# The transfers of value tiles 4 to 7 moved into steps 4 to 7 of the loop, and the first two residual loads put behind step 3

## What is computed

```
xq  = (1 + scale_q) * norm(x)   + bias_q      # scale, bias = silu(cond) @ Wss_q + bss_q
xkv = (1 + scale_kv) * norm(ctx) + bias_kv
q = xq @ Wq + bq;  k, v = split(xkv @ Wkv + bkv)
attn = softmax(q k^T / sqrt(32))               # per head
out = x + (attn v) @ Wp + bp
```

## Time and profile before

| | |
|---|---|
| median of 3 runs | 1062.99 us (1062.55 to 1064.18) |
| the profiled execution's own time | 1062.06 us |
| its span in the profile | 1060.2 us |
| PE busy | 1019.4 us, 96% of the span |
| DVE busy | 989.8 us, 93% |
| POOL busy | 832.3 us, 79% |
| ACT busy | 787.5 us, 74% |
| granted TensorE clock over the span | 0.994 |

### The profile page before, as it was taken

The page is one execution under the profiler, slowest core; times in us unless marked ns, Lnnn a source line. Parts: engine busy times, 40 slices in busy tenths (PEclk is TensorE's granted clock), DMA queues, the critical chain, the costliest instruction groups (busy, mean ns, idle before and its releaser), DMA issues.

```text
span 1060.2 us, 29080 instructions
## 1 busy us (share of the span) xinstructions
PE 1019.4 (96%) x10051; PEld 576.6 (54%) x10051; DVE 989.8 (93%) x1288; ACT 787.5 (74%) x1400; POOL 832.3 (79%) x933
## 2 busy tenths in 40 slices
PE   6999899999999999999999999999999999999965
PEld 2666555555555555555555555555555555555532
DVE  5775899999999999999999999999999999999994
ACT  2564677878787887878787878878787878877552
POOL 2372587979888897979898888979797988889454
PEclk8999999999999999999999999999999999999999
DMA  9231478877777778777777777777777777776775
GB/s 346 102 100 51 99 175 190 178 191 183 182 193 175 184 172 197 184 176 188 194 174 183 189 182 189 169 194 183 177 188 185 183 191 177 184 191 142 160 159 129
DMA packets 382386, 185.19 MB, mean 175 GB/s; under 512 B 324828, under 2 KB 328952, under 8 KB 382344
## 3 DMA queue, kind: packets, MB, share of 16 engines
q1 hardware_dynamic: 382320, 184.66, 71.4%
q10 hardware_dynamic: 24, 0.01, 0.0%
HBM read 77.90 MB, written 33.55 MB: 105 GB/s over the span
## 4 chain that ended last, share of the span: by engine, by line
PE 75%; DMA 7%; SPq 7%; DVE 4%; issue 4%; POOL 2%; ACT 0%; POOLq 0%; DVEq 0%; ACTq 0%
PE ps_q L1442 26%; PE ps_o L1503 26%; PE ps_s L1465 8%; PE ps_v L1487 8%; DMA pt<-p 6%; PE ps_v L1425 4%; SPq L369 3%; SPq L358 2%; DMA cx<-in_ctx_dram 1%; PE ps_v L1296 1%; SPq L334 1%; DVE v L1023 1%; DVE p L1107 0%; DVE cx L932 0%; PE ps_s L1367 0%
## 5 line engine op out<-in xcount | busy, mean ns | idle before, releaser
L527 POOL TENSOR_TENSOR xr<-y,xr 128x512 f32<-128x512 f32 x128 | 163.0, 1273 | 57.5 <-ACT y L667 55.7
L691 ACT CAST p<-ps_t 128x1024 f16<-128x1024 f32 x128 | 129.5, 1012 | 100.0 <-DVE ps_t L1083 98.3
L534 POOL TENSOR_TENSOR half_den<-pr 128x512 f32<-128x512 f32 x128 | 163.4, 1277 | 51.1 <-ACT pr L726 49.0
L503 POOL TENSOR_TENSOR xr<-xr,bp_row 128x512 f32<-128x512 f32 x128 | 163.0, 1273 | 0.8 <-DMA xr<-in_x_dram 0.8
L1091 DVE TENSOR_REDUCE mx<-ps_s 128x16 f32<-128x1024 f32 x128 | 156.8, 1225 | 7.1 <-PE ps_s L1465 2.8
L1107 DVE TENSOR_TENSOR p<-ps_t,p 128x1024 f16<-128x1024 f32 x128 | 156.6, 1223 | 4.0 <-ACT p L691 2.7
L1083 DVE SCALAR_TENSOR_TENSOR ps_t<-pr,ps_v 128x1024 f32<-128x1024 f32 x128 | 155.8, 1217 | 0.3
L1099 DVE TENSOR_TENSOR pr<-ps_s,mx 128x1024 f32<-128x1024 f32 x128 | 155.6, 1215 | 0.1
L726 ACT ACTIVATE pr<-pr,exp_scale 128x1024 f32<-128x1024 f32 x128 | 146.3, 1143 | 10.6 <-DVE pr L1099 10.6
L702 ACT ACTIVATE q_hi<-ps_q,cur_bq 128x512 f16<-128x512 f32 x126 | 86.6, 687 | 89.1 <-PE ps_q L1442 89.1
L1503 PE MATMUL ps_o<-wp_hi,oT_hi 128*128 128x512 f16 x512 | 132.3, 381 | 13.5 <-DVE oT_lo L1058 13.5
(11 more groups left out here) (211 smaller groups left out, 1878.4 us busy)
## 6 DMA issues: line engine op xcount, KB each, us to landing
x_in<-in_x_dram SPq DMA_DIRECT2D x128, 256.0 KB, 3.2
xr<-in_x_dram SPq DMA_DIRECT2D x128, 256.0 KB, 3.1
out_dram<-xr SPq DMA_DIRECT2D x128, 256.0 KB, 3.1
pt<-p SPq DMA_TRANSPOSE x256, 3.2
raw<-in_L_xcond_Wss_kv_dram SPq DMA_DIRECT2D x4, 512.0 KB, 5.9
cx<-in_ctx_dram SPq DMA_DIRECT2D x4, 512.0 KB, 10.9
wss_q_raw<-in_L_xcond_Wss_q_dram SPq DMA_DIRECT2D x4, 512.0 KB, 10.9
raw<-in_L_xcond_Wkv_dram SPq DMA_DIRECT2D x2, 1024.0 KB, 13.8
```

The costliest lines, as they stand in the source:

```text
L503: pool.tensor_tensor(xr[:, s, :], xr[:, s, :], bp_row[:, :], ALU.add).then_inc(xr_ready, 1)
L527: pool.tensor_tensor(xr[:, s, :], y[:, off % 2, :], xr[:, s, :], ALU.add).then_inc(y_ready, 1)
L534: pool.tensor_tensor(half_den[:, :, :], pr[:, off % 2, :, 0:LKV // 2], pr[:, off % 2, :, LKV // 2:LKV], ALU.add).then_inc(half_done, 1)
```

## The change

The transfers of value tiles 4 to 7 leave the stretch in front of SP's loop; each stands now at the end of a step, tile t in step t of batch 0. The first two residual loads, which stood in front of step 3, stand behind it. No instruction is added or removed, and no other engine's program changes.

```
             def step(b, i):
...
                 load_x(b, i + 12)
+                if isinstance(b, int) and b == 0 and i >= KC:
+                    place_values(i)
...
             place_values(3)
             load_x(0, 8)
             load_x(0, 9)
-            place_values(4)
             load_x(0, 10)
             load_x(0, 11)
             load_x(0, 12)
             load_x(0, 13)
-            place_values(5)
             turn_p(0, 0, 0)
             turn_p(0, 0, 1)
-            place_values(6)
             load_x(0, 14)
-            place_values(7)
             sp.wait_ge(wp_ready, 2)
             sp.wait_ge(bv_mm, 1)
+            step(0, 3)
             for f in range(2):
                 load_xr(0, f)
-            for i in range(3, PER):
+            for i in range(4, PER):
                 step(0, i)
```

## The result

The changed kernel takes 1067.78 us (median of 18 runs, 1063.96 to 1073.03); the old one beside it 1062.88 us (18 runs, 1060.09 to 1065.44). The ratio is 1.0047, 95% interval 1.0036 to 1.0057: about 5 us slower, 0.5%, and clear of the noise. The prediction was 1063.5 us, no change, with 1066.0 as the end of its range.

The account below looks back on a forecast made before the run. It took TensorE (busy 96%) as the bound, with `weigh` as clock: -0.8 - 2.6 + 1.2 + 0.5 + 2.0 = +0.3, directly +0.2, plus 0.4 for stalls, about +0.5 us, so 1063.5 us; range 1060.0 to 1066.0.

Parts of the forecast that it names:

- Parts 1 and 2: Prologue: loads ahead of tile 4 gain 0.8 us; clearing SP between transposes of units 0 and 1 removes a 2.61 us wait.
- Part 3: Residual loads behind step 3: POOL starts unit 0's residual at 130.7, 0.2 us later, at no cost by itself.
- Part 4: A block in each of steps 4 to 7, 2.54 us of SP's issuing each, uses up the 3.4 us gained.
- step 6 and the keys: Crossing to batch 1: block until 155.8, keys 155.85, unit 5's transposes 158.6, its `weigh` 163.3; 2.0 us given back.
- one stall at 40%: In SP's chain one stalled issue, worth about 1 us, counted a third to a half: +0.4 us.
- 0.2 us forecast: At `weigh` of unit 5, counted directly: 163.3 against 163.07 before, +0.2 us, stalls not included.
- Rival (b): SP's chain from unit 1's store to unit 5's transposes: two or more stalled issues, +2.7 us, 1065.7; chance 0.15.
- Rival (a): SP's time in steps 4 to 7 is free, so the 3.4 us gain stays: 1059.6 us; chance 0.18.

Follow-up runs that it names:

- all_early_xr_late: all_early with the two residual loads moved from in front of step 3 to behind it; 1061.72 us, ratio 0.9992 to the old kernel.
- all_early: Changed kernel with value tiles 4 to 7 all ahead of unit 0's transposes and residual loads back before step 3; 1059.1 us, ratio 0.9969.
- tiles_6_and_7: Changed kernel with tiles 4 and 5 moved to the prologue and residual loads back before step 3; 1064.37 us, ratio 0.9997.
- changed_again: The changed kernel run once more without any edit, one run; 1071.39 us.
- xr_back: Changed kernel with the two residual loads put back in front of step 3; 1064.8 us, ratio 1.0022 to the old kernel.
- tile_6_early: Changed kernel with value tile 6 alone moved to the prologue; 1062.83 us, ratio 1.0009 to the old kernel.

## Why the prediction was wrong, step by step

**Parts 1 and 2: right.** First transposes at 117.15 (as predicted), `weigh` of unit 0 at 122.75 (122.9), of unit 1 at 130.04 (130.2), its wait of 2.61 us gone.

**Part 3, "this costs nothing by itself": wrong.** It costs 1.8 us alone at unit 6 (all_early_xr_late against all_early), or 1.0 to 1.5 us counted from unit 1 in three traces. I had followed POOL's lateness only to where a block made the transposes late, and not to the keys: even without a block the store of unit 2 holds them back. The landing was mis-sized also: the residual load issued at 127.54 reached POOL at 131.65, 4.1 us later, not 3.05. By that POOL's `add_rows` of units 0 and 1 end at 138.7 and 146.5, not at 137.75 and 145.6. Timeline of POOL of the changed kernel:

```profile
131.65 1.27 POOL L502 TENSOR_TENSOR xr<-xr,bp_row 128x512 f32<-128x512 f32 x1 [2.73 <-DMA xr<-in_x_dram]
...
137.44 1.27 POOL L526 TENSOR_TENSOR xr<-y,xr 128x512 f32<-128x512 f32 x1
...
145.22 1.26 POOL L526 TENSOR_TENSOR xr<-y,xr 128x512 f32<-128x512 f32 x1
```

**Part 4, mechanism right, size too small.** The places of the waits (units 3, 4, 5) are the predicted ones, and for unit 6 almost nothing of its own, also as predicted. The term "step 6 and the keys" was put at a pair issued at 158.6 and `weigh` at 163.3; measured 161.38 and 167.27. Two errors. First, 2.8 us of stalled issues and of the late first store, in a chain that I had described as without free time, but costed with the shortest issue times of the old trace and one stall at 40%. Second, the 4.66 us from a pair's issue to `weigh`, taken from one undisturbed pair, was 5.89 here, 6.25 in tiles_6_and_7. With 0.2 us forecast, 2.8 for SP, 1.2 for the landing and 1.6 for the clock (below) make the 5.8 us at unit 6. The records of DMA packets show what lies in this stretch: the start of the 16 KB packet of the page's instruction queue q8 near this pair (with its length), next to the two landing times of the pair of unit 5 in each trace:

```
old            163.7 us (1.17)   pair issued 158.41, landed after 3.3 and 3.2 us
changed        163.9 us (1.31)   pair issued 161.38, landed after 4.8 and 4.4 us
changed_again  165.9 us (1.01)   pair issued 163.38, landed after 4.5 and 4.1 us
tiles_6_and_7  159.8 us (0.88)   pair issued 155.96, landed after 3.2 and 4.8 us
xr_back        158.3 us (1.11)   pair issued 155.86, landed after 4.5 and 4.2 us
```

In the old trace the pair had landed by 162.9, before the packet of instructions; wherever the pair is late, the packet starts while it is in flight, and what is in flight lands 0.9 to 1.6 us late (in tiles_6_and_7 the first of the two had landed at 159.2). The view of DMA for 164.0 to 166.5 us in the changed kernel shows the engines at a standstill from 164.9 to 166.1, that is, from 1.0 us behind the start of the packet to 0.9 us behind its end (busy share in 40 slices of 0.0625 us):

```profile
DMA  5899999999999900000010000000010019999999
```

That the packet is the cause, is argued from coincidence; no run takes the packets away. The coincidence is a close one, though. Of the 3328 transposes in the 13 traces 146 landed after 4.0 us or more, and for each of them a 16 KB packet of q8 started between 1 us ahead of its issue and its landing. Of the 2492 transposes issued between 217 and 919 us, where no trace has such a packet, none landed that late.

**A term that was missing: the clock.** Windows of the changed kernel (columns as above): the step ahead of the long wait, the wait, the step behind it, the next one.

```profile
156.38:163.74 7.36, 7.36 (x76) 4.10 (x76) 6.17 (x8) 4.69 (x9) 4.62 (x6) 1.00 0.66 182
163.74:167.27 3.53, 0.00 (x0) 0.03 (x1) 1.22 (x1) 1.01 (x1) 1.39 (x3) 1.00 1.20 142
167.27:176.18 8.91, 8.91 (x76) 4.79 (x77) 6.14 (x8) 4.69 (x9) 3.96 (x4) 0.81 0.85 244
176.18:183.47 7.29, 7.29 (x81) 4.09 (x77) 7.25 (x10) 5.61 (x10) 5.29 (x7) 1.00 0.67 152
```

The 76 matmuls of step 8's round take 8.91 us at a granted clock of 0.81 and 7.29 at 1.00: 1.62 us, spent at the lower of the two levels (1.2 in place of 2.4 GHz) after TensorE stood still for 3.53 us. Between 118 and 1010 us it fell in all four traces with a wait of 3.28 us or more (1.62 us over the next step in three of them, 2.68 in xr_back, where the clock read 0.72). Of the ten waits of 2.0 to 2.7 us there only that before unit 0 in changed_again (2.01 us) was followed by it. "TensorE: Matmul & The Clock Gate" in the Trainium skill, Part 1, says that a gate sets this clock by how busy the array has been; that is how the rows read. A wait thus has a price beyond its length, and I had none for it.

**Rival (b), stalled issues,** is what happened to SP, by the mechanism that I gave it; priced at 1065.7 it left out the clock, and the late landing it named without a price. With 0.15 its chance was too low: the old trace has five stalled issues on SP between 98 and 210 us. Rival (a), the gain kept, would have needed a free SP, and all_early, where SP has it, is just that case: 1059.1, against 1059.6.

The sum for the changed kernel against all_early, at unit 110: residual loads 2.1 us (all_early_xr_late, -3.3 to -1.2), block of tile 6 with the fall of the clock 6.0 (tile_6_early, +5.9 to -0.1), and the rest, 9.2 - 8.1 = 1.1 us, tiles 4, 5 and 7; the parts aren't independent, since each makes the same pair of transposes late (tile_6_early, with the late residual loads and tiles 4, 5 and 7, loses 3.2 us).

One reading of the old trace was loose, without effect on the sum: the chain that ended last runs through SP alone from 118 to 129.9 us only; from there to 133.5 it is the transposes' landing.

**The sentence of the Trainium skill**, page "DMA: Bandwidth & Descriptors", that the time to initiate a DMA "is usually small relative to the DMA itself" does not hold here for what matters: an issue takes 0.6 us and one 64 KB move of a value tile lands 2.0 to 3.6 us after it in the changed kernel, but four of them take 2.5 to 3.5 us of SP, and that is what the transposes waited for.

## What to carry to other kernels

When DMAs are moved in a queue, look for the time in which the queue waits anyway, and ask what stands right behind their new place: with the residual loads early in both, the same four tiles leave 3.3 us won at unit 110 in front of the transposes (all_early) and lose 4.0 in the loop (xr_back), most of it for the one block in front of the keys. A queue that another engine's lateness holds back has no use for an early start; move what feeds that engine first (the two residual loads). And where a chain on one queue has no free time, cost it with its mean issue time, stalls included, and add the clock's price, 1.6 us or more here, to every wait of TensorE of some 3 us.

## What the runs showed of the hardware

- Executions of one kernel are longer where the mean granted clock is lower: over 35 timed executions of the old kernel (1059.24 to 1065.99 us) time and clock correlate with -0.91, over another 35 (1059.12 to 1067.09 us) with -0.81. Behind unit 110 one trace of the old kernel lost 2.4 us more than the other.
- With transposes in flight, the DMA engines stood still for some 1.2 us (19 of the 40 slices above show 0 or 1, each is 0.0625 us), beginning 1.0 us behind the start of a 16 KB packet of instructions. In the 13 traces 58 issues of a transpose took over 1.7 us, up to 2.7, where 1.3 is usual; each of them overlaps such a packet or starts within 1 us of its end.
- A transpose lands 3.2 us after its issue undisturbed, and up to 5.2 us after it with such a packet in between (unit 2's in the old trace).
